# An attention and routed-expert block: routing steps on GpSimd, another ScalarE order, and both halves of a unit in one block

## What is computed

```python
xn = layernorm(x)                              # x: 32 x 256 tokens, 128 features, f32
q, k, v = heads of xn @ Wq.T, xn @ Wkv_down.T @ Wk_up.T, xn @ Wkv_down.T @ Wv_up.T
attn = softmax(q k^T / sqrt(32))               # 8 heads of 32, 256 keys per sequence
A = (attn v) @ Wo.T
e = floor(xn . wr + br) mod 8                  # one expert of 8 per token
F = relu(xn @ W1[e] + b1[e]) @ W2[e] + b2[e]   # 128 -> 512 -> 128
out = x + A + F
```

## Time and profile before

| | us |
|---|---|
| median of 3 runs | 508.06 (507.12 to 509.37) |
| the profiled execution: its own time | 513.86 |
| its span | 512.0 |
| busy PE / DVE / POOL / ACT | 459.1 / 418.5 / 378.0 / 346.2 |

### The profile page before, as it was taken

How to read it: one execution, slowest core, us unless ns; L and a number is a source line. 1 busy time by engine, 2 the same in 40 slices (tenths; PEclk the granted TensorE clock), 3 DMA queues, 4 the chain that set the end, 5 groups by cost and what they waited for, 6 DMA issues and landing times.

```text
span 512.0 us, 15093 instructions
## 1 busy us (share of the span) xinstructions
PE 459.1 (90%) x4992; PEld 320.8 (63%) x4992; DVE 418.5 (82%) x898; ACT 346.2 (68%) x864; POOL 378.0 (74%) x387
## 2 busy tenths in 40 slices
PE   1766769899999999997999999997999999999977
PEld 1355435456566465666999999984666656657635
DVE  6878997677998888975788888885698898898865
ACT  3677446666777777775777777765687587677664
POOL 4544266888888888854777777776698888988962
PEclk9985798999999999999999999999899999999999
DMA  8675213444747588599787898844365556756422
GB/s 241 222 168 128 61 52 86 120 103 94 201 118 192 150 235 251 156 261 235 218 270 236 269 276 265 252 132 99 88 138 140 134 127 139 144 108 146 97 73 63
DMA packets 81930, 83.07 MB, mean 162 GB/s; under 512 B 10608, under 2 KB 66384, under 8 KB 81872
## 3 DMA queue, kind: packets, MB, share of 16 engines
q1 hardware_dynamic: 77520, 73.40, 52.8%
q0 software_dynamic: 4352, 8.92, 7.1%
HBM read 38.61 MB, written 18.37 MB: 111 GB/s over the span
## 4 chain that ended last, share of the span: by engine, by line
PE 62%; DVE 15%; DMA 6%; issue 6%; SPq 5%; ACT 4%; POOL 2%; DVEq 0%; ACTq 0%; POOLq 0%
PE psum L1269 9%; PE psum L1234 8%; PE psum L1253 7%; DVE negm L975 6%; PE psum L1392 5%; PE psum L1311 4%; PE psum L1284 4%; PE psum L1375 3%; PE psum L1393 3%; PE psum L1376 3%; PE psum L1377 3%; SPq L324 3%; PE psum L1182 3%; DMA stk<-mT 2%; PE psum L1183 2%
## 5 line engine op out<-in xcount | busy, mean ns | idle before, releaser
L686 ACT ACTIVATE prob<-psum 128x512 f32<-128x512 f32 x256 | 150.1, 593 | 103.9 <-PE psum L1253 82.2
L975 DVE TENSOR_REDUCE negm<-psum 128x2 f16<-128x512 f32 x256 | 170.8, 682 | 46.1 <-PE psum L1234 40.1
L603 POOL TENSOR_TENSOR padd<-prob 128x512 f32<-128x512 f32 x104 | 126.7, 1218 | 36.2 <-ACT prob L686 27.3
L1234 PE MATMUL psum<-stk 96*128 96x256 f16 x512 | 102.4, 282 | 11.6 <-DVE negm L975 10.8
L554 POOL TENSOR_TENSOR padd<-xTl,padd 128x512 f16<-128x512 f32 x71 | 82.2, 1158 | 34.8 <-DVE padd L1087 34.8
L1253 PE MATMUL psum<-stk 97*128 97x256 f16 x512 | 99.1, 277 | 6.8 <-DMA stk<-mT 3.5
L756 ACT ACTIVATE xTl<-psum,xn_all 128x128 f32<-128x128 f32 x284 | 80.9, 368 | 27.6 <-POOL padd L554 17.1
L572 POOL DMA_INDIRECT xsort<-xn_all,pos x64 | 67.2, 1049 | 15.9 <-issue 13.8
L580 POOL DMA_INDIRECT xn_all<-ysort,pos x64 | 65.7, 1026 | 14.0 <-issue 7.5
L1234 PEld LDWEIGHTS psum<-stk 96*128 96x128 f16 x512 | 42.1, 99 | 53.9 <-DVE negm L975 27.1
L1269 PE MATMUL psum<-prob,vt 128*32 128x256 f32 x1024 | 70.5, 394 | 0.6 <-ACT prob L686 0.6
(11 more groups left out here) (167 smaller groups left out, 889.9 us busy)
## 6 DMA issues: line engine op xcount, KB each, us to landing
stk<-split SPq DMA_DIRECT2D x192, 128.0 KB
xn_all<-wsplit SPq DMA_DIRECT2D x71, 258.0 KB, 4.6
xTh<-xsort SPq DMA_DIRECT2D x18, 256.0 KB, 4.3
ysort<-xTh SPq DMA_DIRECT2D x18, 256.0 KB, 4.6
out<-acc SPq DMA_DIRECT2D x15, 256.0 KB
acc<-x SPq DMA_DIRECT2D x3, 1024.0 KB, 8.0
xn_all<-W SPq DMA_DIRECT2D x12, 256.0 KB
wsplit<-xn_all SPq DMA_DIRECT2D x12, 256.0 KB
```

The source lines that it names most:

```text
L603: nc.gpsimd.tensor_tensor(padd[:, bb, hs], prob[:, bb, hs, 0, :], prob[:, bb, hs, 1, :], ALU.add).then_inc(pool_add, 1)
L686: nc.scalar.activation(prob[:, bb, h, :, :].rearrange("p a c -> p (a c)"), bank[st_bank(u, n)], ACT.Exp, scale=SCALE).then_inc(act_exp, 1)
L975: V.tensor_reduce(negm[:, k % 2, col:col + 2], bank[n % 2].rearrange("p (a c) -> p a c", a=2), AX.X, ALU.max, negate=True).then_inc(dve_ma ...
L1234: ins = mm(bank[n % 2][:, qc * T:(qc + 1) * T], stk[0:96, s, 1, h, t0 + qc * P:t0 + (qc + 1) * P], stk[0:96, s, 0, h, t0:t0 + T], start=Tr ...
```

## The change

It has three parts.

- **One block.** `values` and `sums` of half 1 stand behind those of half 0 at n = 7 of the same unit; DVE's `key_add` of heads 6 and 7 (head 7 in the second half) moves from n = 0 of the next unit to n = 7, behind the row maximum and ahead of the residual. The places after the loops, where the last half 1 was finished, go.
- **Routing on POOL.** Counts, tile numbers, offsets and the rows to clear (`tile_counts`, 16 small instructions one behind another, with rounding by adding and subtracting a constant in place of a shift, and a prefix sum in three steps) run on POOL in unit 0 between its second and third addition; two operations on 128 x 512 values (`ranks_moved`) in unit 1 between its second and third. The clearing scatters are placed anew, and the rows of `sel` are made ahead of unit 0.
- **ACT's order in the preparation.** `root(2)` comes one superblock later, `norm(8)` behind `v_copy(0, 0)`, and the table load behind `max_T(0, 7)` at s = 14.

```diff
@@ POOL @@
+            def tile_counts():
+                TT, TS, cast = nc.gpsimd.tensor_tensor, nc.gpsimd.tensor_scalar, nc.gpsimd.tensor_copy
+                pool.wait_ge(dve_rank, 1)
+                cast(upto[:, 1:E + 1], cum[:, :, NC - 1]).then_inc(pool_upto, 1)
+                pool.wait_ge(pool_upto, 1)
+                step(TT(n_e, upto[:, 1:E + 1], upto[:, 0:E], ALU.subtract))
+                step(TS(nt_e, n_e, 1.0 / P, 0.5 - 1.0 / (2 * P), ALU.mult, ALU.add))
+                step(TS(nt_e, nt_e, ROUND, None, ALU.add))
+                step(TS(nt_e, nt_e, ROUND, None, ALU.subtract))
+                step(cast(pre[0][:, 4:4 + E], nt_e))
+                for i in range(3):
+                    step(TT(pre[1 - i % 2][:, 4:4 + E], pre[i % 2][:, 4:4 + E], pre[i % 2][:, 4 - 2 ** i:4 - 2 ** i + E], ALU.add))
+                step(cast(ct_e, pre[1][:, 4:4 + E]))
...
+                step(cast(zpos[:], zposf))
+
+            def ranks_moved():
+                pool.wait_ge(dve_rank, 2)
+                step(nc.gpsimd.tensor_tensor(cum, cum, off_e.unsqueeze(2).broadcast_to([P, E, NC]), ALU.add))
+                nc.gpsimd.tensor_tensor(cum, cum, oh, ALU.mult).then_inc(pool_cum, 1)
...
-                    if u == 0 and n == 6:
-                        expert_rows()
-                    if u == 1 and n % 2 == 1:
-                        if n == 1:
-                            pool.wait_ge(dve_rt, 1)
-                            pool.wait_ge(sp_zero, 16)
-                        for e in range(n - 1, n + 1):
+                    if u == 0 and n == 4:
+                        tile_counts()
+                        pool.wait_ge(sp_zero, 16)
+                    if u == 1 and n in (0, 3):
+                        for e in range(n, n + 3):
                             scatter_zeros(e)
+                    if u == 1 and n == 4:
+                        ranks_moved()
+                    if u == 1 and n == 6:
+                        scatter_zeros(6)
+                        scatter_zeros(7)
@@ ACT, preparation @@
-                if s + 3 < NSB:
+                if s + 3 < NSB and s != 5:
                     act.wait_ge(dve_ln, (s + 3) // 4 + 1)
                     norm(s + 3)
                 if s == 3:
                     k_high(0, 0)
                     q_high(0, 0)
-                    root(2)
                 if s == 4:
                     k_high(1, 1)
                     q_high(1, 1)
+                    root(2)
                 if s == 5:
                     v_copy(0, 0)
+                    act.wait_ge(dve_ln, 3)
+                    norm(8)
...
                     root(3)
-                    nc.scalar.preload_act_table_set("natural_log_exp_and_others")
                 if s == 14:
                     max_T(0, 7)
+                    nc.scalar.preload_act_table_set("natural_log_exp_and_others")
@@ DVE, ranks @@
                 if part == 1:
-                    dve.wait_ge(dve_rank, 1)
-                    step(V.tensor_copy(upto[:, 1:E + 1], cum[:, :, NC - 1]))
-                    step(V.tensor_tensor(n_e, upto[:, 1:E + 1], upto[:, 0:E], ALU.subtract))
+                    dve.wait_ge(pe_rank, 2)
+                    dve.wait_ge(pool_upto, 1)
+                    V.tensor_tensor(cum, bank[5].rearrange("p (e c) -> p e c", e=E), cum, ALU.add).then_inc(dve_rank, 1)
...
@@ DVE, body @@
-                        if n == 0 and not f and not (last and k == 3):
-                            key_add(u - 1, 7, 2 - half)
...
+                        if n == 7 and not (last and k >= 2):
+                            key_add(u, 7, 2 - half)
                         if n == 7 and k % 2 == 1 and not (first and half == 0 and k == 1):
                             residual(it * 2 + k // 2 - 1)
@@ PE, body @@
-                        if n == 2 and half == 0 and first and k == 1:
-                            pe.wait_ge(dve_rank, 2)
-                        if n == 2 and not f:
-                            values(u * 2 - 1, k + 3, 1, it * 2 + (k + 1) // 2 * 2)
-                            sums(u - 1, 1, last and k == 3, half)
...
                         if n == 7:
                             values(u * 2, k, 0, sbu * 2 + 1, u + 2 if nxt else u + 1)
                             sums(u, 0, last and k >= 2, half)
+                            if f and half == 0:
+                                pe.wait_ge(dve_rank, 2)
+                            values(u * 2 + 1, k, 1, sbu * 2 + 2)
+                            sums(u, 1, last and k >= 2, half)
```

More of the change, by code:

```diff
@@ L177, in attention_moe_block @@
         pool_zero = sem("pool_zero")
+        pool_upto = sem("pool_upto")
+        pool_cum = sem("pool_cum")
         act_w = sem("act_w")
@@ L494, in _ @@
             step(nc.gpsimd.tensor_copy(iota_p, iota_pi))
+            for i in range(2):
+                step(nc.gpsimd.memset(pre[i], 0.0))
             def norm(s):
@@ L536, in _ @@
                 norm(s)
-            def expert_rows():
-                step(nc.gpsimd.memset(sel[:], 0.0))
-                for base in (0, -32):
-                    step(nc.gpsimd.affine_select(out=sel[:], in_=sel[:], compare_op=ALU.not_equal, fill=WS,
-                                                 base=base, pattern=[[-1, E], [0, P]], channel_multiplier=1))
+            step(nc.gpsimd.memset(sel[:], 0.0))
+            for base in (0, -32):
+                step(nc.gpsimd.affine_select(out=sel[:], in_=sel[:], compare_op=ALU.not_equal, fill=WS,
+                                             base=base, pattern=[[-1, E], [0, P]], channel_multiplier=1))
+            def tile_counts():
[11 more added lines that the diff above has]
+                step(cast(ct_e, pre[1][:, 4:4 + E]))
+                step(TT(off_e, ct_e, nt_e, ALU.subtract))
+                step(TS(off_e, off_e, float(P), None, ALU.mult))
+                step(TT(off_e, off_e, upto[:, 0:E], ALU.subtract))
+                step(TT(zposf, off_e, upto[:, 1:E + 1], ALU.add))
+                step(TS(zposf, zposf, iota_p, None, ALU.add))
+                step(cast(zpos[:], zposf))
[3 more added lines that the diff above has]
+                nc.gpsimd.tensor_tensor(cum, cum, oh, ALU.mult).then_inc(pool_cum, 1)
             def scatter_zeros(e):
@@ L1038, in body @@
                             row_max(u + w, wn, k + w)
-                        if f and half == 0 and n >= 4:
-                            ranks((0, 1, 3, 2)[n - 4])
-                        if first and half == 0 and k == 1 and n in (0, 1, 4, 6):
-                            ranks({0: 4, 1: 5, 4: 6, 6: 7}[n])
+                        if f and half == 0 and n in (4, 7):
+                            ranks(n // 7)
+                        if first and half == 0 and k == 1 and n == 7:
+                            ranks(2)
                         if half == 0 and isinstance(u, int):
@@ L1122, in _ @@
                     q_low(1, 1)
[L1123 removed]
+                    scale_bias(2)
                 if s == 5:
@@ L1144, in _ @@
                 body(it, 0, False, False)
-            key_add(NU // 2 - 1, 7, 2)
             for t in range(2):
@@ L1448, in _ @@
             tok_T(1)
-            values(NU - 1, 3, 1, NU // 2)
-            sums(NU // 2 - 1, 1, False, 0)
             hidden(0)
@@ L1482, in _ @@
             body(NIT - 1, 1, False, True)
-            values(2 * NU - 1, 3, 1, NU)
-            sums(NU - 1, 1, True, 1)
             for bb in range(2):
```

33 lines of the change are left out of this document (8 added, 25 removed).

## The result

The changed kernel takes 552.93 us, median of 4 runs (550.66 to 555.28), beside 507.59 (505.19 to 509.37) of the kernel before: a ratio of 1.0876, 95% interval 1.0839 to 1.0912. The forecast was 548 with a range from 530 to 562. The profiled execution took 555.28, its span 553.4, which is 41.4 more than the span of the kernel before; the sum of the prediction was 39.8. By the medians the change is 45.3, since the profiled execution of the kernel before (513.86) was 6.3 over its median and this one 2.4.

The account below looks back on a forecast made before the run. The prediction saw TensorE almost without a gap in the second half (10.0 us a unit) and POOL nearly full in the first. Its terms summed to +39.8 on the median 508.06, about 548 us, range 530 to 562.

Parts of the forecast that it names:

- preparation: Ahead of unit 0: ACT's idle time at `root(2)` goes, the table load costs 1.28; -2.0 us, between -4 and 0.
- routing, units 0 and 1: POOL's 16 steps and `ranks_moved` make `sums` of units 0 and 1 wait; unit 2 starts 3.3 us later.
- block, first half, units 2 to 14: Units 2 to 14 take 149.0 us against 136.0, +13.0; unit 2's scatter waiting for the clearing adds 0.9.
- seam: Unit 15's half 1 is done ahead of the experts' first transpose, whose load has more room: -2.0 us.
- unit 16: POOL starts late after the experts, so unit 17 starts at 358.7 and not 357.5: +1.2 us.
- POOL's ring: Units 17 to 29: exponential 0, POOL's four additions, `sums`, next exponential 0; 11.92 us a unit, +24.9 us together.
- last two units and end: No POOL additions in the last two units: +0.5 us, between -1 and +2.
- ACT's ring: From `sums` through exponentials 0 to 7 and `values` of half 1: 10.4 us in even units, 11.3 in odd.
- rival 3: TensorE idles over 1 us in every unit and its clock falls: +32, 580 us; chance 0.08.
- Rival 1: Only TensorE's work counts: 31 pairs of matmul mode changes saved at 0.2 give -6.2; 500 us; chance 0.07.
- Rival 2: POOL keeps up, ACT's ring holds in the second half too: +10.9 in place of +24.9, 534 us; chance 0.10.
- Rival 4: The rings are shorter than read and everything cancels, or parts don't do what they say: 506 to 511; chance 0.05.

Follow-up runs that it names:

- e3_act: The kernel before with ACT's new order in the preparation alone, DVE's statistics and `scale_bias(2)` turned to match: 507.45 us, ratio 0.9994.
- e1_block: The kernel before with the joined block alone, routing left on DVE and ACT's order as before: 553.63 us, ratio 1.0919.
- e5_late: The changed kernel with `late_low` and `tile_experts` moved from n = 6 to n = 7, behind `key_add` and the residual: 547.04 us, ratio 1.0765.
- e2_rest: The changed kernel with the block undone, half 1 finished at n = 2 of the next unit again: 508.66 us, ratio 1.0003.
- e4_gather: The changed kernel with POOL's gather of n = 5 moved behind the addition of head 6: 544.05 us, ratio 1.0704.

## Why the prediction was right

By its own steps, on the profiled executions (sum forecast 39.8, measured 41.4):

| step | forecast | measured |
|---|---|---|
| preparation | -2.0 | -1.0 (not told from 0) |
| routing, units 0 and 1 | +3.3 | +4.9 |
| block, first half, units 2 to 14 (with 0.9 for unit 2) | +13.9 | +12.3 |
| seam | -2.0 | -0.6 (not told from 0) |
| unit 16 | +1.2 | +1.4 |
| POOL's ring, units 17 to 29 | +24.9 | +27.9 |
| last two units and end | +0.5 | -3.6; against other runs +0.6 to +0.9 |

The mechanism was right: the joined block closes rings, POOL's sets the second half, and DVE's late steps set units 6 to 9, 11 and 13. Two terms of the sum were not: the gains of 2.0 each in the preparation and at the seam, which no run shows. By the medians the sum is 5.5 short of 45.3.

- **POOL's ring.** Forecast 11.92, measured 12.15 a unit, and the kernel with the gather moved shows that it is the cause: its wait for POOL gives way to a shorter one for DVE and the unit falls. Two of its terms were too small by 0.1 to 0.2: the addition of head 6 took 0.96 and not 0.73, since DVE's `key_add` now runs beside it, and from `sums` to the next exponential it was 2.03 and not 1.92. The 27.9 has a stretch of low clock on either side: 2.3 us in the changed kernel, and in the kernel before unit 17 took 12.0 with a clock of 0.50 from 358 to 361, where `e3_act` took 10.4 without. From two executions with the clock at 1.00 throughout, `e1_block` and `e3_act`, it is 155.7 - 128.6 = 27.1.
- **ACT's ring** in the first half: 10.66 for unit 2, 11.35 for 3, 10.42 for 4, 11.21 for 5 where 10.4 and 11.3 were forecast, 12.2 to 12.4 for 7, 9, 11 and 13 (12.1). The even units behind `late_low` were too high (10.99 to 11.01 for 10 and 12, where 11.4 was forecast). The plain even ones came out right in part by luck. Exponential 7 ends 7.02 after exponential 0, not 7.38, and `values` doesn't wait for it; in unit 14 and, in `e5_late`, in 6, 8 and 14 `sums` waits 0.15 to 0.17 for DVE's addition instead, which brings the same 10.4.
- **Routing.** The 16 small steps on POOL, from the end of the wait at 62.64 to 67.69, took 5.05 us where 5.1 was forecast by the variance step's 0.317. `sums` of unit 0 was at 69.09 (70.0), that of unit 1 at 85.11 (85.9). What was missing is behind it: TensorE had idled 4.76 us, the granted clock was 0.50 from 84 to 91 us, and from `sums` to exponential 0 it took 3.37 us, not 1.92. This is rival 3 in one place, and units 17 and 29 are two more; from unit 3 to 15 and from 18 to 28 the clock stayed at 1.00, and there the rival fell. (By its own signs the prediction was wrong in unit 29: POOL's fourth addition was ready before TensorE, and the clock fell.) Even so the routing costs nothing against the block alone: there units 0 and 1 take 31.5 us (54.58 to 86.08), and 34.3 in the changed kernel, but unit 2 takes 13.3 and not 10.7, and unit 3 begins at 99.4 in the one and 99.1 in the other. So the forecast's +3.3 and +0.9 came out near, but under the wrong name: the block lengthens the start by as much without POOL's steps.
- **Preparation and seam** were each given a gain of 2.0, and neither shows. The first exponential comes at 54.0 to 56.1 in the five runs with the old order and at 53.1 to 55.6 in the nine with the new. From the first exponential of unit 15 to that of 16 it is 123.8 to 128.1 in the five runs with half 1 at head 2, and 124.3 to 125.7 in the seven with it joined. At the seam the experts' first transpose still waits for its load, and comes 10.8 after the first exponential of unit 15, where it was 11.3:

```profile
247.54 0.41 PE L1380 MATMUL psum<-ident,xTh 128*128 128x128 f32 x2 [0.80 <-DMA xTh<-xsort]
```

- **The end** seems wrong in sign: from the first exponential of unit 30 to the end of the span it is 20.8 us, before 24.4. But that one execution of the kernel before was slow there. `e3_act` and `e2_rest`, which run its code behind unit 16, take 20.0 and 20.2. Of `e3_act`, whose span is 504.2 (L1255 the transposed scores):

```profile
484.29 1.09 ACT L686 ACTIVATE prob<-psum 128x512 f32<-128x512 f32 x2 [0.84 <-PE psum L1255]
```

So the end costs 0.6 to 0.9, as forecast. These 4 us and the 1.6 of unit 17 are about the 6 by which that execution lay over the median, and why the 41.4 of the spans is less than the 45.3 of the medians. That the sum of 39.8 stood so near the 41.4 was in part luck.

Rival 1, TensorE's work alone, had its gain: from `sums` of half 0 to `values` of half 1 the step is 0.43 (455.93 to 456.36), without a change of mode. It is not on the path, since TensorE then waits 0.56 for POOL. Rival 2 is the kernel in which POOL keeps up; the kernels with POOL's ring shortened came close to it (544, then 538 with DVE's wait out too, where 534 was given). Rival 4 holds for the two parts beside the block.

## What to carry to other kernels

Before work is joined into one group, ask what stood between its halves: here 4 us of other matmuls covered three engines' last steps, and joining the halves closed a ring through each of them. Sum each ring from one first event to the next; the longest sets the rate, and when it is cut the next one is often only half a microsecond shorter. And a block that uses one engine alone starves the engines it feeds; in the kernels with half 1 at head 0 or 1 they were late afterwards, which is the likely reason that the loss was larger than the ring by itself told. Before a small step of a sum is called right or wrong, look at it in a second execution of the same code: here one execution of the kernel before hid 4 us at its end.

## What the runs showed of the hardware

A VectorE operation with two operands in SBUF is stretched beside POOL's additions, and these are stretched by it. `expert_sum` takes 0.69 with POOL free, 1.28 on average at head 6 of the kernel before, and 1.70 in the row of `e4_gather` above. POOL's addition of head 6 by form, in the kernel before and in the changed one, where `key_add` has moved beside it:

```profile
L603 POOL TENSOR_TENSOR padd<-prob 128x256 f32<-128x256 f32 x14 | 10.3, 736 | 0.3
```

```profile
L633 POOL TENSOR_TENSOR padd<-prob 128x256 f32<-128x256 f32 x14 | 13.2, 945 | 1.1 <-ACT prob L719 0.9
```

The `key_add` in question, 0.72 where one with POOL free takes 0.41:

```profile
456.62 0.72 DVE L1030 TENSOR_TENSOR padd<-prob 128x256 f32<-128x256 f32 x1
```

The Trainium skill's page GPSIMD Engine Reference, Specifications, says that the two engines share their interface to SBUF and contend for operations with two SBUF inputs; the trace agrees, and this is most of the 0.2 us a unit by which POOL's ring was longer than forecast.

Not expected, and open, is what holds up the signals of TensorE's second `sums` and of the groups behind it by 1.6 to 2.6 us in nine units of one kernel, told above.
